# Shared experts' 704 features as 384 and 320 instead of twice 352, with the last 64 gates and ups in one chunk; a slot table padded in rows, and expert loads spread over the output phase

## The reference

```python
# x: (2, 1024, 512): 2048 tokens of 512 features, float32
def _L0_attn_ref(x, Wq, Wk, Wv, Wo):            # 16 heads of 32
    Q, K, V = (split_heads(x @ W.T) for W in (Wq, Wk, Wv))
    S = jnp.einsum('bhqd,bhkd->bhqk', Q, K) * scale
    P = jax.nn.softmax(jnp.where(causal, S, NEG), axis=-1)
    O = jnp.einsum('bhqk,bhkd->bhqd', P, V)
    return O.transpose(0, 2, 1, 3).reshape(b, t, D) @ Wo.T

def _L0_ffn_ref(x, ...):                        # 8 experts of 352, top 2 of 8 by 2 of 4 groups
    def _mlp(x, gw, uw, dw):
        return jax.nn.silu(x @ gw.T) * (x @ uw.T) @ dw.T
    # routed: each token's two experts, weighted
    # shared: shared_gate_w, shared_up_w (704, 512), shared_down_w (512, 704)
    return routed.reshape(orig_shape) + _mlp(x, shared_gate_w, shared_up_w, shared_down_w)

xn = _layernorm(x, axis=-1)
x = x + _L0_attn_ref(xn, ...) + _L0_ffn_ref(xn, ...)
```

## Time and profile before

| | us |
|---|---|
| median of three runs | 1050.87 |
| lowest, highest | 1046.09, 1958.02 |
| the profiled execution | 1046.42 |
| its span | 1044.7 |

### The profile page before, as it was taken

The page is one execution under the profiler, slowest core; times in us unless marked ns, Lnnn a source line. Parts: engine busy times, 40 slices in busy tenths (PEclk is TensorE's granted clock), DMA queues, the critical chain, the costliest instruction groups (busy, mean ns, idle before and its releaser), DMA issues. The chain is left out here.

```text
span 1044.7 us, 18885 instructions
## 1 busy us (share of the span) xinstructions
PE 981.6 (94%) x5176; PEld 808.7 (77%) x5177; DVE 725.4 (69%) x1436; ACT 678.2 (65%) x1419; POOL 533.8 (51%) x573
## 2 busy tenths in 40 slices
PE   5999988999999999999999999988879999999994
PEld 4767877787787877777777877766679999999993
DVE  6741332667687788888898888753467777777771
ACT  3332211278788897888888878871167777777771
POOL 0010840768788877876666766751013444434421
PEclk9999989999999999999999999999899999999997
DMA  6989897644787867969868778538889545465432
GB/s 202 331 320 383 228 205 266 204 134 96 192 159 172 174 138 177 202 143 268 247 199 247 206 247 199 171 117 290 294 283 310 100 91 123 93 173 89 77 59 38
DMA packets 136491, 199.69 MB, mean 191 GB/s; under 512 B 63088, under 2 KB 81776, under 8 KB 132816
## 3 DMA queue, kind: packets, MB, share of 16 engines
q1 hardware_dynamic: 126064, 177.88, 59.8%
q0 software_dynamic: 9760, 20.49, 10.6%
q10 hardware_dynamic: 576, 0.26, 0.2%
HBM read 117.11 MB, written 73.08 MB: 182 GB/s over the span
## 5 line engine op out<-in xcount | busy, mean ns | idle before, releaser
L1448 POOL TENSOR_TENSOR prob_lo<-prob,prob_hi 128x512 fp32r<-128x512 f32 (+2 forms) x320 | 329.7, 1048 | 127.1 <-ACT prob_hi L1492 114.8
L1485 ACT ACTIVATE prob<-ps_s 128x512 f32<-128x512 f32 (+3 forms) x384 | 188.1, 490 | 70.9 <-PE ps_s L1729 50.0
L1492 ACT ACTIVATE prob_hi<-prob 128x512 fp32r<-128x512 f32 (+3 forms) x384 | 199.4, 520 | 12.4 <-ACT row_stage L1466 12.4
L1581 DVE CUSTOM_DVE_ANT_0 ps_m<-ps_m,causal 128x384 f32<-128x384 f32 (+3 forms) x256 | 125.4, 497 | 55.3 <-PE ps_m L1700 48.5
L2140 DVE TENSOR_TENSOR rw_lo<-gu_sb,rw_hi 128x704 fp32r<-128x704 f32 x156 | 135.8, 892 | 34.7 <-ACT rw_hi L2072 32.6
L2072 ACT ACTIVATE rw_hi<-gu_sb 128x704 fp32r x156 | 123.5, 794 | 32.0 <-issue 21.8
L2045 POOL DMA_INDIRECT out<-work,slot_table x39 | 64.5, 1654 | 155.3 <-ACT work L2102 94.1
L1724 PE MATMUL ps_s<-qs,ks 97*128 97x512 f32 (+3 forms) x384 | 136.3, 355 | 3.2 <-DMA qs<-max_rows 2.2
L1700 PE MATMUL ps_m<-ks,qs 96*128 96x512 f32 (+3 forms) x384 | 131.3, 342 | 5.6 <-DVE maxima L1581 5.5
L1747 PE MATMUL ps_o<-prob_hi,vs 128*66 128x512 f32 (+3 forms) x384 | 130.0, 339 | 1.3 <-POOL prob_lo L1448 1.3
L1749 PE MATMUL ps_o<-prob_lo,vs 128*66 128x512 f32 (+3 forms) x384 | 129.3, 337 | 0.0
(11 more groups left out here) (207 smaller groups left out, 2358.3 us busy)
## 6 DMA issues: line engine op xcount, KB each, us to landing
xt<-xt_blocks SPq DMA_DIRECT2D x7, 2048.0 KB, 8.5
v_rows<-work SPq DMA_DIRECT2D x16, 512.0 KB, 3.1
xt_blocks<-xt SPq DMA_DIRECT2D x4, 2048.0 KB, 11.3
qk_hi<-work SPq DMA_DIRECT2D x8, 1024.0 KB, 4.5
qk_lo<-work SPq DMA_DIRECT2D x8, 1024.0 KB, 7.3
qs<-qk_hi SPq DMA_DIRECT2D x64, 128.0 KB
ks<-qk_hi SPq DMA_DIRECT2D x64, 128.0 KB
vs<-v_rows SPq DMA_DIRECT2D x32, 256.0 KB
```

The source lines that it names most:

```text
L1448: nc.gpsimd.tensor_tensor(prob_lo[:, s % NPL, 0:w], prob[:, s % NP, 0:w], prob_hi[:, s % NPH, 0:w].bitcast(F32), ALU.subtract).then_inc(lo ...
L1485: nc.scalar.activation(prob[:, s % NP, 0:w], bank("score", s)[:, 0:w], ACT.Exp, scale=SCALE).then_inc(exp_done, 1)
L1492: nc.scalar.activation(prob_hi[:, s % NPH, 0:w], prob[:, s % NP, 0:w], ACT.Copy).then_inc(hi_ready, 1)
L1581: nc.vector.tensor_tensor_reduce(ps_m[s % NM][:, 0:w], ps_m[s % NM][:, 0:w], causal[:, TBW - w:], 1.0, MASKED, ALU.add, ALU.max, maxima[:, ...
```

## The change

- **Chunks.** The halves become parts of 384 and 320: `SHARED` cuts the first into 128, 128, 128 and the second into 128, 128, 64. The last chunk is mixed: its 64 gate and 64 up columns lie side by side in `sg_hi`/`sg_lo` (`second_places`), one group of 12 matmuls makes both in one bank, and `hidden` takes the ups from partitions 64 to 127. Units of the second part have 96 matmuls instead of 108, so the banks' roles flip from unit to unit (`BANK`, `y_bank`). Waits on `up_done` count only separate up groups (`ups`). All fillers' due steps are worked out again. `tanh` is gone: tanh is written to `gated` and updated in place, ScalarE waiting for the `hid` of the chunk before. `add` is due no later than the step that needs its bank.
- **Weights.** `sgate`, `sup` and `sdown` are laid out whole; the shared weights' tiles are 384 wide; GpSimd splits the down weights in one pair of operations instead of two.
- **Slot table.** The spare rows are made as 39 rows of 128 slots (`pads`), and stored in whole rows of 1 KB, instead of 8 bytes at a time from `slot_table`.
- **Output phase.** The rows of `out` for the first two tiles are loaded in the attention phase (`load_first_tokens` into `y_first`). The first two experts' loads are spread: gate, up and the two parts of down at steps 4, 5, 6, 7 and 8, 9, 10, 11.
- **Norm phase.** wv is loaded behind x tile 1, not ahead of it.
- **Places.** Some tiles move: `score` and others into space freed, `y_tile` is given back before the routed phase.

```diff
+SHARED = [[(0, 128), (128, 128), (256, 128)], [(0, 128), (128, 128), (256, 64)]]
+PART_AT = [0, 3 * P]
...
-FIRST_AT = [5, 9]
+FIRST_AT = [(4, 5, 6, 7), (8, 9, 10, 11)]
...
+def load_matrix(eng, e, n, matrix, gu_sb, expert_loaded):
+    eng.dma_start(gu_sb[:, e * KC:(e + 1) * KC, n * F:(n + 1) * F],
+                  matrix[e * KC:(e + 1) * KC].rearrange("k p f -> p k f")
+                  ).then_inc(expert_loaded[e % len(FIRST_AT)], 16)
...
+def load_down_part(eng, e, part, down_dram, d_ring, down_loaded):
+    n, w, at = e % DOWN_SLOTS, FCH[-1][1], part * len(FCH)
+    eng.dma_start(d_ring[:, n, at:at + 2, :].bitcast(F32), down_dram[e, :, part, 0:2, :]
+                  ).then_inc(down_loaded[n], 16)
+    eng.dma_start(d_ring[0:w, n, at + 2, :].bitcast(F32), down_dram[e, 0:w, part, 2, :]
+                  ).then_inc(down_loaded[n], 16)
...
# norm_phase, SP
-                    if t == 1:
+                    if t == 2:
+
                         for k in range(KC):
                             sp.dma_start(wv_raw[:, k, :], wv[:, k, :]).then_inc(wv_loaded[k], 16)
...
# project_phase
-                        sp.dma_start(slots_dram.rearrange("(j p) a -> p j a", p=P),
-                                     slot_table[:, :, :]).then_inc(pads_stored, 16)
+                        sp.dma_start(slots_dram.rearrange("(j p) a -> j p a", p=P),
+                                     pads[:, :, :]).then_inc(pads_stored, 16)
...
# attend_phase
-    UNITS = NSH * NTB
+    UNITS = 2 * NTB
     GROUP = 3 * KC
-    UP_END = [2 * GROUP * (k + 1) for k in range(NF)]
-    PER_UNIT = UP_END[-1] + 4 * 3 * NF
+    GATE_END, UP_END = [], []
+    for part in range(2):
+        ends = [0]
+        for k in range(NF):
+            ends += [ends[-1] + GROUP, ends[-1] + (1 if is_mixed(part, k) else 2) * GROUP]
+        GATE_END.append(ends[1::2])
+        UP_END.append(ends[2::2])
+    PER_UNIT = [up_end[-1] + 4 * 3 * NF for up_end in UP_END]
+    BEGIN = [sum(PER_UNIT[n // NTB] for n in range(unit)) for unit in range(UNITS + 1)]
...
+    BANK = [sum(is_mixed(n // NTB, NF - 1) for n in range(unit)) % 2 for unit in range(UNITS)]
+
+    def y_bank(unit, q):
+        return (BANK[unit] + is_mixed(unit // NTB, NF - 1) + q) % 2
...
+    def ups(n):
+
+        return sum(not mixed(c) for c in range(n))
...
-    TANH_AT, GATE_AT = chunks_at(GROUP, 1), chunks_at(GROUP, 2)
-    HIDDEN_AT, HIDDEN_HI_AT, HIDDEN_LO_AT = [chunks_at(2 * GROUP, lag) for lag in (1, 2, 3)]
+    TANH_AT, GATE_AT = [chunks_at(GATE_END, lag, lag) for lag in (1, 2)]
+    HIDDEN_AT, HIDDEN_HI_AT, HIDDEN_LO_AT = [chunks_at(UP_END, lag, lag + 1) for lag in (1, 2, 3)]
...
+                def load_first_tokens():
+
+                    sp.wait_ge(acc_stored, 64 * (UNITS - NTB + 1))
+                    for t in range(OUT_AHEAD):
+                        sp.dma_start(y_first[:, t, :], out[t * P:(t + 1) * P, :]
+                                     ).then_inc(x_loaded[t], 16)
...
                         wait(act, gated_ready, n)
-                        nc.scalar.activation(tanh[0:w, :], ps_f[0][0:w, :], ACT.Tanh,
+                        wait(act, hid_ready, n)
+                        nc.scalar.activation(gated[0:w, :], ps_f[BANK[n // NF]][0:w, :], ACT.Tanh,
                                              scale=0.5).then_inc(tanh_ready, 1)
...
-                        dve.wait_ge(up_done, n + 1)
+                        dve.wait_ge(up_done, ups(n + 1))
                         dve.wait_ge(gated_ready, n + 1)
                         wait(dve, hid_lo_ready, n)
-                        nc.vector.scalar_tensor_tensor(hid[0:w, :], gated[0:w, :], 0.5,
-                                                       ps_f[1][0:w, :], ALU.mult,
-                                                       ALU.mult).then_inc(hid_ready, 1)
+                        up_of = ps_f[bank][w:2 * w, :] if mixed(n) else ps_f[1 - bank][0:w, :]
+                        nc.vector.scalar_tensor_tensor(hid[0:w, :], gated[0:w, :], 0.5, up_of,
+                                                       ALU.mult, ALU.mult).then_inc(hid_ready, 1)
...
-                    last = nc.tensor.matmul(ps_f[part][0:w, :],
-                                            (w_hi, w_lo, w_hi)[term][:, kc, f0:f0 + w],
+                    last = nc.tensor.matmul(ps_f[(BANK[unit] + part) % 2][:, :],
+                                            (w_hi, w_lo, w_hi)[term][:, kc, f0:f0 + P],
                                             xt[:, (0, 0, 1)[term], kc, :], start=(j == 0),
                                             stop=(j == GROUP - 1))
...
-                        if q < 2:
-                            pe.wait_ge((gated_ready, hid_ready)[q], NF * (unit + 1))
+                        if q >= 2:
+                            pe.wait_ge(y_added, 4 * unit + q - 1)
+                        elif mixed(chunks - 1):
+                            pe.wait_ge(hid_ready, chunks - 1 + q)
                         else:
-                            pe.wait_ge(y_added, 4 * unit + q - 1)
+                            pe.wait_ge((gated_ready, hid_ready)[q], chunks)
...
# out_phase
                     t = U * i + c
+                    if t < R:
+                        return
                     wait(sp, added, t - U + 1)
...
-                    if isinstance(t, int) and t in FIRST_AT:
-                        e = FIRST_AT.index(t)
-                        load_expert(sp, e, gate, up, gu_sb, expert_loaded)
-                        load_down(sp, e, down_dram, d_ring, down_loaded)
+                    for e, at in enumerate(FIRST_AT):
+                        for n, matrix in enumerate((gate, up)):
+                            if t == at[n]:
+                                load_matrix(sp, e, n, matrix, gu_sb, expert_loaded)
+                        for part in range(2):
+                            if t == at[2 + part]:
+                                load_down_part(sp, e, part, down_dram, d_ring, down_loaded)
...
-                    nc.vector.tensor_tensor(y_sum[:, c, :], ps_y[c % R][:, :], y_tile[:, c, :],
+                    tokens = y_first if t < R else y_tile
+                    nc.vector.tensor_tensor(y_sum[:, c, :], ps_y[c % R][:, :], tokens[:, c, :],
                                             ALU.add).then_inc(added, 1)
```

More of the change, by code:

```diff
@@ L44, with is_mixed @@
 FCH = [(0, 128), (128, 128), (256, 96)]
+FSH = NSH * F
+SHARED = [[(0, 128), (128, 128), (256, 128)], [(0, 128), (128, 128), (256, 64)]]
+PART_AT = [0, 3 * P]
+assert PART_AT[1] + sum(w for _, w in SHARED[1]) == FSH
+def is_mixed(part, k):
+    return SHARED[part][k][1] < P
 NORM_SLOTS, YS = 4, 4
-FIRST_AT = [5, 9]
+FIRST_AT = [(4, 5, 6, 7), (8, 9, 10, 11)]
 ROW_SLOTS, GS = 8, 4
@@ L217, in moe_attention_kernel @@
         with nc.sbuf_tensor("gu_sb", [P, E * KC, 2 * F], F32) as gu_sb, \
[L218 to L221, removed]
+                nc.sbuf_tensor("d_ring", [P, DOWN_SLOTS, 2 * len(FCH), D], F32R) as d_ring:
+            with nc.sbuf_tensor("y_tile", [P, YS, D], F32) as y_tile:
+                out_phase(nc, finish, wo_hi, wo_lo, out_hi, out_lo, a_hi_ready, a_lo_ready, gate, up, down_dram, ident, work, gu_sb, d_ring, out, y_tile, y_first, y_stored,
+                          slot_table, xn_dram, gathered, passed, expert_loaded, w_loaded, x_loaded)
             finish_ctx.close()
@@ L981, in step_cost, with chunks_at @@
         return cost
-    FILL = fill_counts([step_cost(s) for s in range(ALL)], UNITS * PER_UNIT, 0, STEPS + AHEAD, 228.0)
+    FILL = fill_counts([step_cost(s) for s in range(ALL)], BEGIN[-1], 0, STEPS + AHEAD, 228.0)
     FILLED = [sum(FILL[:s]) for s in range(ALL + 1)]
     def step_of(unit, m):
-        return next(s for s in range(ALL) if FILLED[s + 1] > PER_UNIT * unit + m)
-    def chunks_at(after, lag):
+        return next(s for s in range(ALL) if FILLED[s + 1] > BEGIN[unit] + m)
+    def chunks_at(ends, lag, lag_mixed):
@@ L992, in chunks_at @@
         found = {}
         for n in range(UNITS * NF):
-            found.setdefault(step_of(n // NF, 2 * GROUP * (n % NF) + after - 1) + lag, []).append(n)
-        return found
-    TANH_AT, GATE_AT = chunks_at(GROUP, 1), chunks_at(GROUP, 2)
-    HIDDEN_AT, HIDDEN_HI_AT, HIDDEN_LO_AT = [chunks_at(2 * GROUP, lag) for lag in (1, 2, 3)]
+            unit, k = divmod(n, NF)
+            found.setdefault(step_of(unit, ends[unit // NTB][k] - 1)
+                             + (lag_mixed if mixed(n) else lag), []).append(n)
@@ L1044, in attend_phase @@
         d_raw = sbuf("d_raw", [P, NF, D])
-        tanh = sbuf("tanh", [P, TBW])
         gated = sbuf("gated", [P, TBW])
@@ L1183, in load_xt @@
                 def load_xt(unit):
-                    wait(sp, up_done, NF * unit)
+                    wait(sp, gate_done, NF * unit)
+                    wait(sp, up_done, ups(NF * unit))
                     sp.dma_start(xt[:, :, :, :].bitcast(F32), xt_dram[unit % NTB]
@@ L1781, in down @@
                     term = m % 3
```

(10 more changed lines are left out.)

173 lines of the change are left out of this document (88 added, 85 removed).

## The result

The changed kernel takes 1043.24 us (median of 12 runs, 1037.97 to 1044.77) where the kernel before took 1052.89 beside it: a ratio of 0.9904, 95% interval [0.9879, 0.9929]. That is about 10 us less. The ratio is taken without the one run of the kernel before that took 1958.02 us. 21.5 were predicted; 1043 lies outside the range of 1016 to 1035, and on the side of "within 2%".

What follows compares the result with a forecast made beforehand. The prediction took TensorE, at 94% of the span, as the bound. Its gains of 7.8, 7.2, 5.5 and 1.0 us sum to 21.5, taking 1046.4 to 1025 us, range 1016 to 1035.

Steps and rivals of the forecast that it cites:

- part 1: Attention phase: 48 fewer shared-expert matmuls, 11.0 us of TensorE, of which 7.8 us show, bounds 4 and 11.
- 88% of the slow stretch: Attention phase, 364 to 671 us: VectorE's share was to reach 88% or more, from 87%, if the saving came.
- The product of the mixed chunk: Attention phase: down matmuls might wait once or twice for VectorE's product; taken as nothing, up to 2.8 us.
- Part 2: Projection phase: storing the padded slot table in 1 KB rows gives back 7.2 us, bounds 5 and 7.5.
- The rival that the store wasn't the blocker: Projection phase: heads and stores alone block the queues, so the new table layout gives nothing; 1032 us, chance 0.05.
- Part 3: Output phase: spreading the first two experts' loads over four tiles each gains 5.5 us, bounds 2 and 9.3.
- The byte count: Output phase: 10.2 MB up to tile 12's load take 29 us at 350 GB/s, so some 3.8 us stay lost.
- The rival "slower": Output phase: late loads make TensorE wait over 1.40 us per tile and the clock fall repeatedly; 1066 us, chance 0.03.
- That `y_first` gives nothing: Output phase: loading the first two tiles' rows early gains nothing, since TensorE did not wait for the first sums.
- Part 4: Start: loading wv behind x tile 1 gains 1.0 us, bounds 0 and 2, first projection matmul near 13 us.

Runs made afterwards that it cites:

- e6: e1 without the mixed chunk: gates and ups in separate matmuls again, 864 in all; 1036.51 us, ratio 0.9877 to the kernel before.
- e1: The changed kernel with the mixed chunk's down matmuls over 128 rows, the lower 64 rows of weights zero; 1027.49 us, ratio 0.9794 to the kernel before.
- e4: e1 with the six loads of each of the first two experts issued together again; 1032.64 us, ratio 0.9842 to the kernel before.
- e7: e1 with wv loaded ahead of x tile 1 again; 1032.69 us, ratio 0.9827 to the kernel before.
- e3: The changed kernel with the slot table stored as before, 8 bytes at a time; 1042.74 us, ratio 0.9935 to the kernel before.
- e5: The kernel before with the down matmuls of each unit's last chunk over 65 rows instead of 96; 1052.85 us, ratio 1.0031.
- e8: The changed kernel once more, unedited, for a second profile; 1042.31 us, ratio 0.9936 to the kernel before.
- e9: The kernel before with all 288 shared down matmuls over 64 rows; 1107.41 us, ratio 1.0553.

## Why the prediction was wrong

**The step that failed** is in part 1: "The first half's third chunk has 128 rather than 96 rows, with the same 512 columns, so no time." It followed the last chunk of the first half up and not that of the second half down, to 64, and took a matmul's price from its columns alone. "What the mixed chunk adds: nothing in ScalarE's or VectorE's count" looked at the engines that read the chunk, not at TensorE, which contracts over it. The term left out measured 11.6 us. 31 groups of 0.29 us are 9.0 of it; that the other 2.6 are the slow-clock stretch behind such groups (last section) fits, but isn't shown. The diff showed it (`(256, 64)`), but no row of before could have priced it: none of its matmuls in that phase is under 96 rows.

A rule would have raised the question. The Trainium skill ("TensorEngine Tiling (Array Packing)", section "Key Properties") says that changing the tiling mode, "not just tile", drains TensorE, and its section "When to Use Tiling" names a contraction of up to 64 rows as the case for row tiling. That a plain matmul over 64 rows counts as such a change of mode, the page doesn't say; no run here shows it, and it stays a reading. The trace agrees with it on the border (64 costs, 65 doesn't) and on a cost at the change; the page gives no price, here 0.29 us for the way there and back, and doesn't tell of the 0.11 between the first and the second of a group.

**Part 1, the matmuls taken away:** predicted 7.8 (4 to 11), measured 9.0 in the medians and 6.4 to 11.5 in the phase (e6 against e1, e4 and e7). That confirms the size, but it doesn't tell 7.8 from the full 48 x 0.23 = 11.0. Where it came differs from the prediction: from the phase's first matmul to its 141st score block the three profiles are 1 to 4 us shorter than e6's, where 4.0 were foreseen, from there to the 371st 6 to 8, where half of 6.5 was, so VectorE didn't keep half there. VectorE's share was read as a bound, but with the saving in place VectorE simply did its work in less time: 81.5% of the phase (419.63 of 514.89) instead of 80.7%. The test set for it, 88% of the slow stretch, wasn't met (263.31 of 307.4 us, 86%, in e1, where it was 87%; counted between the 141st and the 371st score block 85 to 86% in before, e6 and the three) though the saving came: that test was a bad one. The product of the mixed chunk, taken at nothing with up to 2.8 us, holds TensorE up once for 1.32. The attention phase was named at 515; it is 514.9 in e1, but 517.5 in the mean of the three.

**Part 2, the slot table:** predicted 7.2 (5 to 7.5), measured 6.0 in the phase by e3, 7.8 by the means of six profiles each (4 to 11 by the single ones). Its signs are there: no slice at 5 GB/s, no clock below 1.00 from 128 to 154, ScalarE's evacuations 2.7 to 2.8 us apart but for one of 3.9. The rival that the store wasn't the blocker falls.

**Part 3, the output phase:** predicted 5.5 (2 to 9.3), measured 5.0 to 5.7 in the phase, 3.7 by e4 against e1 in the phase and 5.1 in the medians. 37.16 us against 37 from tile 3 to tile 15, so 3.6 us are still lost where 3.8 were estimated. The byte count held: the sums slip to 4.7 us late at tile 12 (750.00, where 2.80 us a tile from 720.08 give 745.28). PE's own waits don't grow (0.64, 0.34, 0.44), and the clock is 1.00 from 712 us on. The rival "slower" falls by its own condition: no gap reached 1.40 (the longest in e1 is 1.00). That `y_first` gives nothing isn't decided: e4 has it and takes 57.4, where the five profiles of the old output phase took 57.6 to 59.4.

**Part 4, the start:** predicted 1.0 (0 to 2), measured 1.3 (e7), and 2.0 between the means of six profiles each. The first projection matmul is at 12.52, 1.6 earlier than before.

With the failed term repaired the rest of the sum holds: 21.5 predicted, and e1 is 22.3 below the kernel before in the same series (1049.82 - 1027.49). That it holds this closely is in part luck, as single terms are known to 2 or 3 us only. The reasoning on queues was right; what was wrong is a price not looked for.

## What to carry to other kernels

When a change cuts a dimension anew, write down the new height, width and length of every matmul it touches, the contraction of the consumer too, and look for any that contract over only 64 rows among taller ones (fewer than 64 weren't measured): here each such excursion costs 0.29 us, more than a whole matmul of 512 columns. Rows that take the height above 64 cost nothing in the spacing (e5, and e1 with zero rows), so pad the weights; if that can't be, put the short ones next to each other, since from the third on they cost nothing. A saving in matmuls on an engine that is 97% busy showed for the most part (about 9 of 11.0 us) even where another engine stands at 87%. And take more than one profile of a phase: the attention phase differed by 5 us between e1 and e4 and by 10 between after and e3, with the same code in it.

## What the hardware showed unexpectedly

**How long TensorE waited doesn't decide by itself whether the clock falls.** PE's timeline of after, then its table by stretches around it:

```profile
549.78 0.39 PE L1863 MATMUL ps_f<-sd_hi,hid_lo 64*128 64x512 f32 x1
551.16 0.47 PE L1767 MATMUL ps_m<-ks,qs 96*128 96x128 f32 x1 [0.99 <-DVE maxima L1648]
...
554.69 0.63 PE L1814 MATMUL ps_o<-prob_hi,vs 128*66 128x512 f32 x1
555.12 0.63 PE L1816 MATMUL ps_o<-prob_lo,vs 128*66 128x512 f32 x1
```

```profile
553.00:559.00 6.00, 6.00 (x16) 3.70 (x16) 2.11 (x6) 2.44 (x5) 3.01 (x3) 0.50 0.87 235
...
535.00:565.00 30.00, 29.01 (x124) 20.38 (x123) 22.02 (x45) 20.60 (x49) 17.98 (x17) 0.83 0.73 219
```

After a wait of 0.99 us the granted clock is 0.50 (1.2 GHz), and matmuls are 0.43 apart. It is so in all three profiles with the 64-row matmuls (after, e8, e3: waits of 0.97 to 0.99, 6.8 to 10.2 us at half clock). In the three with 128 rows (e1, e4, e7) the corresponding wait is 1.57 and the clock stays at 1.00; e1's timeline, then its table for the same stretch:

```profile
543.06 0.33 PE L1772 MATMUL ps_m<-ks,qs 96*128 96x128 f32 x1 [1.57 <-DVE maxima L1653]
```

```profile
541.00:547.00 6.00, 4.43 (x26) 3.47 (x25) 5.80 (x15) 3.70 (x8) 3.96 (x4) 1.00 1.00 325
...
535.00:565.00 30.00, 28.25 (x154) 22.42 (x153) 26.48 (x58) 24.78 (x58) 20.27 (x20) 1.00 0.82 248
```

154 matmuls in those 30 us of e1 against 124 of after. e8 has the same stretch at 0.83 with 120. That the 64-row matmuls ahead of the wait play a part here fits these six profiles; it is argued and not shown, since no run changed the wait alone, and they aren't needed for a fall. In e9 the clock falls near 208 us, amid groups of 64 rows (PE's timeline):

```profile
208.50 0.69 PE L1792 MATMUL ps_f<-sd_hi,hid_hi 64*128 64x512 f32 x1 [0.52 <-DVE hid_lo L1628]
```

But it falls near there in e5 too, which has no matmul under 65 rows. e5's timeline and table, then the same stretch of before:

```profile
203.88 0.50 PE L1792 MATMUL ps_f<-sd_hi,hid_hi 65*128 65x512 f32 x1 [0.68 <-DVE hid_lo L1628]
...
207.03 0.79 PE L1792 MATMUL ps_f<-sd_hi,hid_hi 128*128 128x512 f32 x1 [1.12 <-DVE y_acc L1637]
```

```profile
206.00:213.00 7.00, 5.97 (x15) 4.82 (x16) 2.83 (x9) 0.00 (x0) 0.00 (x0) 0.52 0.29 113
```

```profile
206.00:213.00 7.00, 5.87 (x30) 4.66 (x29) 3.85 (x13) 0.71 (x2) 0.00 (x0) 1.00 0.48 185
```

Before has the same two waits there (0.68 and 1.13) and keeps its clock. The same holds where the attention phase starts, behind a wait of TensorE of 2.73 or 2.74 us in every profile: the clock falls there in five of the six with the new table store, and in one of the six with the old one. Of three profiles with one code in this phase it falls in e4 and e7 and not in e1, which is 1.6 us ahead of them by that. So the clock can fall behind the same wait and the same matmuls in one run and not in another; what else decides isn't shown here. After has one more such place at 307 us, behind a wait of 1.87 us for a DMA, ahead of any 64-row matmul; 3 of the 4.4 us between the two profiles of after lie there, in the wait and in the 3.4 us at half clock behind it.
